# Linear attention and a gated block: the value projection per token becomes a product of moments, and biases become rows of weights

## The chip, the core and the metric

One NeuronCore of a Trainium2 runs the whole kernel. The metric is the device time of one execution in microseconds. TensorE is called PE in the profile, VectorE DVE, ScalarE ACT, GpSimd POOL, and SyncE (which issues the transfers here) SP. The engines run their own instruction streams in order and wait for each other on semaphores.

## What is computed

```python
xn = layernorm(x)                                   # x: 8 batches x 512 tokens x 128
q, k, v = split(xn @ Wqkv + bqkv, 3)
qp, kp = elu(q) + 1, elu(k) + 1
kv = einsum('bsd,bse->bde', kp, v)                  # one 128x128 matrix a batch
attn = (qp @ kv) / (qp . sum_s kp + 1e-6)
x1 = layer_norm(xn + attn, g1, b1)
s = layer_norm(x1 + (silu(x1 @ Wg + bg) * (x1 @ Wu + bu)) @ Wd + bd, g2, b2)

gf = global_net(mean_s xn)                          # three small layers on the mean over tokens
out = xn
for _ in range(3):                                  # coupling cycles
    tf = coupling_net(out)                          # 128 -> 128 -> 64 -> 32 -> 1, gelu
    c = 0.1 + adaptive_range * (0.7 * gf + 0.3 * tf - 0.5) * 2
    out = out + c * twist(out)                      # twist: quarters of the features swapped, some negated
result = x + s * silu(out)
```

## The kernel before

Everything stays on chip between the first load and the last store. A batch is four tiles of 128 tokens, so there are 32 tiles. Each engine has one hand-written order of work, and counters (semaphores, one for each product) tie them together. There are three stages.

**Token stage (to about 67 us).** For batch b, TensorE projects q for the whole batch (`project_q`, L890 to L894) and then, tile by tile (`project_tokens`, L903 to L906), k, v and two products with the first coupling weight, 512 columns in all. Float32 operands are split into a high and a low part, so each product is three matmuls, and the biases of k and v are one more matmul against a matrix of ones (L905). ScalarE reads each tile's bank in `token_tile`: exp for k (L373), the copy of v (L376), the copy of the other two quarters (L377). VectorE makes the k feature (`feature_k`, L578). TensorE then adds k feature times (v, 1) into one bank (`sum_kv`, L915), two tiles behind the projection. VectorE copies the sum (`copy_kv`, L585), TensorE multiplies the q features with it (`numerator`, L924), VectorE divides and adds xn (`attend`, L601), then takes the statistics of the sum (L527, L533) and negates the mean (`negate_mean`, L539). GpSimd adds epsilon (L228), takes the power -0.5 (L229) and forms minus mean times rstd (L240). ScalarE normalises (`norm_1`, L385) for batches 0 to 4, GpSimd (`norm_x1`, L257) for batches 5 to 7, and GpSimd multiplies with g1 into x1g (`scale_x1`, L265). For batches 6 and 7 that multiplication stands in GpSimd's order behind `s_pair` (L280, L281), four pairs of long products that belong to the coupling stage. TensorE transposes x1n (`transpose_x1`, L870 in the profile, as all transposes). Three banks serve the tiles in turn, so the projection of tile n waits for the k feature of tile n-3.

ScalarE's order within batch b is: exp of q; for each tile its `token_tile`; `norm_1` of two tiles of batch b-3 behind tiles 0 and 2; the high part of the next batch's transposed xn (`hi_x`, L360) behind tile 1; `hi_x1` at the end. The high and low parts of the transposed xn also accumulate its sum over tokens, from which the mean for the global net comes (L777).

**Coupling stage (to about 128 us).** Twelve slots, a slot being two batches in one of the three cycles: layers 1 to 4 on TensorE with gelu on ScalarE, then the coefficient (`coupling`, L625) and the next layer's input (`next_r`, L637, eight VectorE instructions) on VectorE. The second cycle of a slot reads what `s_pair` wrote.

**Second block (to the end).** For each batch, gate and up products (L1014 to L1016), silu on ScalarE (L446), their product on VectorE (L663), the down product (`down`, L1026) with a bias matmul in front of each tile (L1024, L1039), the residual with x1g and its statistics (L672, L527 to L539), the norm's scalars on GpSimd (L228 to L240), the norm on ScalarE (L454), three products of `gate_rows` on GpSimd (L313 to L317), `o3` on VectorE (L650), and `finish` (L698, L699) one or more batches behind. g1 is multiplied into the gate and up weights (L804), b1 and bd are in the bias matmul.

SP issues all loads in one order at the start: x of batch 0, the columns, the small weights, the first weights, x of batches 1 and 2, the rows, the gate and up weights, the down weights, x of batches 3 to 7. Each is spread over 128 partitions.

## Time and profile before

| | us |
|---|---|
| median of 3 runs | 209.87 |
| lowest and highest | 209.31, 210.67 |
| span of the profiled execution, first to last instruction | 208.3 |

| engine | busy us | share | instructions |
|---|---|---|---|
| TensorE matmul | 171.9 | 83% | 982 |
| VectorE | 168.9 | 81% | 535 |
| ScalarE | 116.5 | 56% | 288 |
| GpSimd | 135.7 | 65% | 220 |

The span lies 1.6 us under the median; what is around it (launch and end) is in the run's time and not in the span. In the timeline a row gives the start of an instruction and how long it was in its engine. Instructions of one engine overlap by their latency, so the price of one more in a full queue is the distance from its start to the next start, not its duration. A bracket at the end gives the idle time before the row and what ended it. PEclk is the TensorE clock granted, 1.00 being 2.4 GHz and 0.50 being 1.2 GHz.

### The profile page before, as it was taken

Reading aid. Unit: us, or ns where it says so; the run is one execution under the profiler, and the core shown is the slowest. Engines: PE = TensorE matmul, PEld = TensorE weight load, DVE = VectorE, ACT = ScalarE, POOL = GpSimd, SP = SyncE. Lnnn points to the kernel's source line nnn. Section 1 sums busy time; section 2 is a strip of 40 time slices with the busy share of each in tenths; the row PEclk is TensorE's granted clock in tenths of the full one; section 3 lists DMA queues with packets and bytes.
Section 4 is the critical chain, followed back from the end, with each engine's and each line's share of the span. In section 5 each row is a group of like instructions: output and inputs, shape, how many; then the busy total and the mean of one; then the engine's idle time right before and its main releaser. Section 6 shows DMA issues by size and latency. Waiting matters only on the chain.

```text
span 208.3 us, 3423 instructions
## 1 busy us (share of the span) xinstructions
PE 171.9 (83%) x982; PEld 119.9 (58%) x982; DVE 168.9 (81%) x535; ACT 116.5 (56%) x288; POOL 135.7 (65%) x220
## 2 busy tenths in 40 slices
PE   0399999999999899685959998669999979797900
PEld 0266776878677745342334545448788758585900
DVE  4865699999899945999995705984999999999864
ACT  2337687899888569545326886232374545343420
POOL 0284788799945994578671279981568466483981
PEclk9999999999999889979557999957999999999975
DMA  6950000000000000000000000000001011010112
GB/s 133 312 215 0 0 5 0 2 5 0 0 0 5 2 0 3 0 0 0 0 0 0 3 0 2 3 0 3 0 0 50 3 50 50 0 52 3 50 50 101
DMA packets 3330, 5.74 MB, mean 28 GB/s; under 512 B 496, under 2 KB 1136, under 8 KB 3312
## 3 DMA queue, kind: packets, MB, share of 16 engines
q1 hardware_dynamic: 3312, 5.52, 8.1%
q8 instruction: 8, 0.13, 0.3%
q14 instruction: 10, 0.08, 0.1%
HBM read 3.43 MB, written 2.10 MB: 27 GB/s over the span
## 4 chain that ended last, share of the span: by engine, by line
PE 51%; DVE 23%; ACT 8%; POOL 8%; issue 4%; DMA 2%; SPq 1%; DVEq 0%; ACTq 0%; POOLq 0%
DVE r_tok L637 9%; PE bank L1026 8%; DVE xn_tok L650 8%; PE bank L870 6%; PE bank L954 5%; PE bank L1014 4%; PE bank L1015 3%; PE bank L1016 3%; POOL rstd L229 3%; PE bank L966 2%; DMA r_tok<-in_w_first 2%; PE bank L903 2%; PE bank L906 2%; PE bank L904 2%; PE bank L915 2%
## 5 line engine op out<-in xcount | busy, mean ns | idle before, releaser
L228 POOL TENSOR_SCALAR ve<-mv 128x4 f32<-128x4 f32 (+1 forms) x25 | 5.1, 206 | 41.6 <-DVE nm L539 40.7
L1014 PE MATMUL bank<-x_hi,ffn_hi 128*128 128x512 f32 (+1 forms) x48 | 21.5, 448 | 9.2 <-DVE pq L663 8.2
L446 ACT ACTIVATE pq<-bank,bffn 128x512 f32<-128x512 f32 (+1 forms) x24 | 15.8, 680 | 21.4 <-PE bank L1016 21.4
L650 DVE SCALAR_TENSOR_TENSOR xn_tok<-tx_tok,ab,xn_tok 128x128 f32<-128x128 f32 x32 | 26.6, 888 | 0.0
L229 POOL TENSOR_TENSOR rstd<-ve,minus_half 128x4 f32<-128x4 f32 (+1 forms) x25 | 24.9, 998 | 2.1
L1026 PE MATMUL bank<-wd,pq 128*128 128x128 f32 x168 | 24.8, 295 | 0.0
L409 ACT ACTIVATE q_stage<-bank,col 128x512 f32<-128x512 f32 x24 | 16.4, 687 | 14.0 <-PE bank L870 13.4
L1026 PEld LDWEIGHTS bank<-wd,pq 128*128 128x128 f32 x168 | 22.5, 203 | 0.2
L663 DVE SCALAR_TENSOR_TENSOR pq<-bank,bffn,pq 128x512 f32<-128x512 f32 (+1 forms) x24 | 17.8, 745 | 4.5 <-ACT pq L446 4.2
L1015 PE MATMUL bank<-x_lo,ffn_hi 128*128 128x512 f32 (+1 forms) x48 | 19.4, 405 | 0.0
L1016 PE MATMUL bank<-x_hi,ffn_lo 128*128 128x512 f32 (+1 forms) x48 | 19.2, 401 | 0.0
L870 PE MATMUL bank<-small,r_tok 128*128 128x128 f32 x64 | 12.6, 330 | 7.7 <-DVE r_tok L637 7.7
L625 DVE SCALAR_TENSOR_TENSOR cpl<-tt,gain,base 128x8 f32<-128x8 f32 x12 | 6.7, 562 | 13.0 <-ACT tt L430 13.0
L637 DVE SCALAR_TENSOR_TENSOR r_tok<-pq,cpl 128x128 f32<-128x128 f32 x32 | 16.8, 594 | 0.1
L1014 PEld LDWEIGHTS bank<-x_hi,ffn_hi 128*128 128x128 f32 (+1 forms) x48 | 8.7, 182 | 14.3 <-DVE pq L663 10.6
L954 PE MATMUL bank<-q_stage,small 128*64 128x512 f32 x48 | 16.1, 755 | 0.0
L906 PE MATMUL bank<-first_hi,xT_lo 128*128 128x512 f32 x32 | 15.9, 497 | 0.0
L454 ACT ACTIVATE pq<-pq,nmr,rstd 128x128 f32<-128x128 f32 x28 | 11.5, 483 | 7.4 <-POOL nmr L240 7.4
L903 PE MATMUL bank<-first_hi,xT_hi 128*128 128x512 f32 x32 | 15.3, 479 | 0.0
L870 PEld LDWEIGHTS bank<-small,r_tok 128*128 128x128 f32 x64 | 8.5, 168 | 11.9 <-DVE r_tok L637 8.9
L373 ACT ACTIVATE ek<-bank,minus_one 128x128 f32<-128x128 f32 x32 | 12.1, 378 | 4.3 <-PE bank L906 3.1
L418 ACT ACTIVATE h<-bank,col 128x256 f32<-128x256 f32 x24 | 10.1, 470 | 7.7 <-PE bank L954 7.7
(134 smaller groups left out, 492.7 us busy)
## 6 DMA issues: line engine op xcount, KB each, us to landing
x_tok<-in_x SPq DMA_DIRECT2D x8, 256.0 KB, 6.4
out<-pq SPq DMA_DIRECT2D x7, 256.0 KB, 2.0
r_tok<-in_w_ffn SPq DMA_DIRECT2D x1, 341.0 KB, 6.3
r_tok<-in_w_first SPq DMA_DIRECT2D x1, 320.0 KB, 4.9
out<-pq SPq DMA_DIRECT2D x2, 128.0 KB, 1.8
small<-in_w_small SPq DMA_DIRECT2D x1, 242.0 KB, 4.1
row<-in_rows SPq DMA_DIRECT2D x1, 192.0 KB, 5.8
wd<-in_w_down SPq DMA_DIRECT2D x1, 192.0 KB, 6.3
```

The lines of the kernel that those rows point to most:

```text
L229: return pool.tensor_tensor(rstd[i][:, b, ts], ve[i][:, b, ts], minus_half[:, ts], ALU.pow)
L637: ins = dve.scalar_tensor_tensor(out=r_tok[:, n], in0=pq[:, n, 1], scalar=cpl[:, s, i // TILES, i % TILES:i % TILES + 1], in1=pq[:, n, 0] ...
L650: last = dve.scalar_tensor_tensor(out=xn_tok[:, b, t], in0=tx_tok[:, b, t], scalar=ab[:, j, 3, i:i + 1], in1=xn_tok[:, b, t], op0=ALU.mult ...
L663: dve.scalar_tensor_tensor(out=hid[b % 2][0:m, c], in0=ps_up[n % 2][0:m], scalar=bffn[0:m, CHUNKS + c:CHUNKS + c + 1], in1=sg[n % 2][0:m], ...
L870: last = pe.transpose(dst[:, t * P:(t + 1) * P], src[:, t], eye)
L903: pe.matmul(dst[:], hi, first_hi[:, 0:4 * D], start=True, stop=False)
L906: pe.matmul(dst[:], lo, first_hi[:, 0:4 * D], start=False, stop=True).then_inc(k_ps, 1)
L954: last = pe.matmul(ps_h2[s % 2][64 * par:64 * par + 64, :], sm("cn_w2"), h1[:, s % 2, par], start=True, stop=True)
L1014: pe.matmul(dst[n % 2][0:m], ffn_hi[:, w], x1_hi[:, b], start=True, stop=False)
L1015: pe.matmul(dst[n % 2][0:m], ffn_hi[:, w], x1_lo[:, b], start=False, stop=False)
L1016: pe.matmul(dst[n % 2][0:m], ffn_lo[:, w], x1_hi[:, b], start=False, stop=True).then_inc(done, 1)
L1026: last = pe.matmul(dst[:, t * P:(t + 1) * P], hid[b % 2][0:m, c, t * P:(t + 1) * P], wd[0:m, c], start=False, stop=(c == CHUNKS - 1))
```

## The change

- Value projection: v is no longer projected for each token. `project_tokens` has 384 columns (k and two coupling products) and the bias matmul 128. `sum_m` accumulates, for each batch, the product of xn (features 1 to 127 and a column of ones) with the k features (and a column of ones), one matmul a tile as before. Then VectorE copies this moment (`copy_m`), TensorE multiplies it with the prepared value weights (`project_kv`, one matmul a batch) and ScalarE copies the result (`copy_kv`), which stands in ScalarE's order behind tile 2 and its `norm_1`.
- The value weights are prepared once on VectorE (`value_weights`, at the end of batch 0): first row subtracted (xn sums to zero over its features), mean over outputs subtracted, so that the first norm's input has mean zero. The same for the first weights of the global net, which read the sum over tokens from the moment.
- The first norm is then a scale only. ScalarE scales for batches 0 to 4; VectorE makes x1g in one pass for batches 5 to 7 (`norm_x1`), and the x1n and x1g work of those batches leaves GpSimd. x1g is what is transposed, so the gate and up weights need no scaling. GpSimd loses the epsilon (all norms) and the product of mean and rstd (first norm); VectorE adds epsilon, which replaces the negated mean in norms 0 and 1 and is one more instruction in norm 2.
- bd and b1 become two rows of the down weights' last chunk (87 rows for 85), against ones that GpSimd writes into the hidden tiles; the bias matmuls of `down` go.
- Loads: the first weights in two transfers; five transfers for the value and global weights, four of them over 127 partitions and one a row of 128 single elements, placed ahead of the rows; the down weights in four, one over 85 partitions and two of them such rows.
- k features have four buffers for three; the accumulation of sums in `hi_x` and `lo_x` goes.

```diff
-                act.activation(xT_hi[:, b % 2], ps_xT[:], ACT.Identity,
-                               accum_out=sum_hi[:, b:b + 1]).then_inc(xT_hi_ready, 1)
+                act.copy(xT_hi[:, b % 2], ps_xT[:]).then_inc(xT_hi_ready, 1)
...
-                act.copy(v1[:, n % 3, 0:D], ps_k[n % 3][:, D:2 * D]).then_inc(v_ready, 1)
-                act.copy(pq[:, n].rearrange("p a d -> p (a d)"), ps_k[n % 3][:, 2 * D:4 * D]).then_inc(pq_ready, 1)
+                act.copy(pq[:, n].rearrange("p a d -> p (a d)"), ps_k[n % 3][:, D:3 * D]).then_inc(pq_ready, 1)
+
+            def copy_kv(b):
+                act.wait_ge(kv_ps, b + 1)
+                if b >= 2:
+                    act.wait_ge(num_ps, b - 1)
+                act.copy(kv_sb[:, b % 2], ps_kv).then_inc(kv_ready, 1)
...
                         norm_1(b - 3, (t, t + 1))
                     if t == 1 and b + 1 < BATCHES:
                         hi_x(b + 1)
+                    if t == 2 and b >= 1:
+                        copy_kv(b - 1)
...
-            def sum_kv(n):
+            def sum_m(n):
...
-                pe.matmul(ps_kv[:, 0:D + 1], kf[:, n % 3], v1[:, n % 3], start=(t == 0),
-                          stop=(t == TILES - 1)).then_inc(kv_ps, 1)
+                pe.matmul(ps_m, xn_ext[:, b, t, 1:D + 1], kf[:, n % KF], start=(t == 0),
+                          stop=(t == TILES - 1)).then_inc(m_ps, 1)
+
+            def project_kv(b):
+
+                pe.wait_ge(m_ready, b + 1)
...
+                pe.matmul(ps_kv, m_sb[:, b, 0:D], wv[:], start=True, stop=True).then_inc(kv_ps, 1)
...
-                    if n >= 2:
-                        sum_kv(n - 2)
+                    if t <= 1 and b >= 1:
+                        sum_m(n - 2)
                     if t == 1 and b + 1 < BATCHES:
                         transpose_x(b + 1)
-                    if t == 3 and b >= 1:
-                        numerator(b - 1)
...
+                    if t == 2 and b >= 1:
+                        project_kv(b - 1)
+                    if t == 3:
+                        sum_m(n - 3)
+                        sum_m(n - 2)
+                        if b >= 1:
+                            numerator(b - 1)
...
+            def value_weights():
+
+                dve.wait_ge(rest_cleared, 1)
+                dve.wait_ge(rest_loaded, 80)
+                link(dve.tensor_tensor(rest_raw, rest_raw, rest_base, ALU.subtract))
+                dve.tensor_copy(gw1[:], rest_raw[:, D:])
+                link(dve.bn_stats(st_v[:], rest_raw[:, 0:D]))
+                link(dve.bn_aggr(mv_v[:], st_v[:]))
+                dve.wait_ge(small_loaded, 16)
+                dve.tensor_copy(wv[:, D:D + 1], eye[:, P - 1:P])
+                dve.tensor_scalar(wv[:, 0:D], rest_raw[:, 0:D], mv_v[:, 0:1], None, ALU.subtract).then_inc(wv_ready, 1)
...
+            def norm_x1(b):
...
+                    last = dve.scalar_tensor_tensor(out=x1g[:, b, t], in0=u1[:, b % 2, t],
+                                                    scalar=rstd[1][:, b, t:t + 1], in1=row_g1,
+                                                    op0=ALU.mult, op1=ALU.mult)
...
-            for b in (BATCHES - 2, BATCHES - 1):
-                scale_x1(b)
...
-                link(pool.tensor_scalar(ve[i][:, b, ts], mv[i][:, b, ts, 1], 1.0, LN_EPS, ALU.mult, ALU.add))
...
+            sp.wait_ge(rest_cleared, 1)
+            gc = slice(SMALL_AT["gc_w1"], SMALL_AT["gc_w1"] + SMALL["gc_w1"])
+            sp.dma_start(rest_raw[0:P - 1, 0:D], w_first[1:P, D:2 * D]).then_inc(rest_loaded, 16)
+            sp.dma_start(rest_raw[P - 1:P, 0:D], as_row("bv"), allow_slow_non_contiguous=True).then_inc(rest_loaded, 16)
+            sp.dma_start(rest_raw[0:P - 1, D:], w_small[1:P, gc]).then_inc(rest_loaded, 16)
+            sp.dma_start(rest_base[0:P - 1, 0:D], w_first[0:1, D:2 * D].to_broadcast([P - 1, D])).then_inc(rest_loaded, 16)
+            sp.dma_start(rest_base[0:P - 1, D:], w_small[0:1, gc].to_broadcast([P - 1, NREST - D])).then_inc(rest_loaded, 16)
...
-                    pe.matmul(dst[:, t * P:(t + 1) * P], ones_bf[:, 0:P], bias3[:, 3 * D:4 * D], start=True, stop=False)
```

## Rows read from the trace of the kernel before

**Rows 1.** Busy time by window: busy us (instructions) of each engine, PEclk, DMA share, GB/s

```profile
40.00:50.00 10.00, 10.00 (x65) 7.49 (x63) 9.52 (x49) 9.27 (x31) 9.05 (x18) 1.00 0.01 3
```

**Rows 2.** Timeline, TensorE, batch 4 of the token stage: start us, us, instruction

```profile
39.09 0.40 PE L903 MATMUL bank<-first_hi,xT_hi 128*128 128x512 f32 x1
...
39.91 0.39 PE L915 MATMUL bank<-v,kf 128*128 128x129 f32 x2
...
43.71 1.06 PE L924 MATMUL bank<-kv_sb,q_stage 128*128 128x129 f32 x8
44.60 0.60 PE L870 MATMUL bank<-small,x1n 128*128 128x128 f32 x4
...
45.97 0.40 PE L903 MATMUL bank<-first_hi,xT_hi 128*128 128x512 f32 x1
```

**Rows 3.** Timeline, ScalarE, the same batch

```profile
40.11 0.37 ACT L373 ACTIVATE ek<-bank,minus_one 128x128 f32<-128x128 f32 x1
40.37 0.26 ACT L376 COPY v<-bank 128x128 f32<-128x128 f32 x1
40.52 0.39 ACT L377 COPY pq<-bank 128x256 f32<-128x256 f32 x1
40.78 0.89 ACT L385 ACTIVATE x1n<-u,nmr,rstd 128x128 f32<-128x128 f32 x2
41.57 0.37 ACT L373 ACTIVATE ek<-bank,minus_one 128x128 f32<-128x128 f32 x1
...
42.22 0.64 ACT L360 ACTIVATE xT_hi<-bank 128x512 fp32r<-128x512 f32 x1
...
42.80 0.41 ACT L373 ACTIVATE ek<-bank,minus_one 128x128 f32<-128x128 f32 x1
```

**Rows 4.** Timeline: TensorE at the start of batches 1 and 3

```profile
19.29 0.40 PE L903 MATMUL bank<-first_hi,xT_hi 128*128 128x512 f32 x1
...
32.20 0.39 PE L903 MATMUL bank<-first_hi,xT_hi 128*128 128x512 f32 x1
```

**Rows 5.** Timeline, VectorE: statistics of batch 3, last copy_kv, two gaps behind the stage

```profile
19.38 0.86 DVE L527 BATCH_NORM_STATS2 st<-x_tok 128x6 f32<-128x128 f32 x4
...
66.62 0.29 DVE L585 COPY kv_sb<-bank 128x129 f32<-128x129 f32 x1 [0.37 <-PE bank L915]
...
76.18 0.69 DVE L617 TENSOR_TENSOR x_lo<-bank,x_hi 128x512 fp32r<-128x512 f32 x1 [1.90 <-ACT x_hi L392]
...
79.06 0.23 DVE L625 SCALAR_TENSOR_TENSOR cpl<-tt,gain,base 128x8 f32<-128x8 f32 x1 [2.06 <-ACT tt L430]
```

**Rows 6.** Timeline, coupling slots 4 and 5: VectorE, then GpSimd, then TensorE

```profile
102.44 6.40 DVE L637 SCALAR_TENSOR_TENSOR r_tok<-pq,cpl,r_tok 128x128 f32<-128x128 f32 x8
...
109.02 2.19 DVE L637 SCALAR_TENSOR_TENSOR r_tok<-pq,cpl,r_tok 128x128 f32<-128x128 f32 x8
...
104.77 2.62 POOL L265 TENSOR_TENSOR x1g<-x1n,row 128x512 f32<-128x512 f32 x2
...
107.85 1.11 PE L870 MATMUL bank<-small,r_tok 128*128 128x128 f32 x4 [2.37 <-DVE r_tok L637]
...
113.00 0.64 PE L870 MATMUL bank<-small,r_tok 128*128 128x128 f32 x4
```

**Rows 7.** Timeline, second block: GpSimd's norm scalars and VectorE's finish

```profile
164.33 0.19 POOL L228 TENSOR_SCALAR ve<-mv 128x4 f32<-128x4 f32 x1 [3.28 <-DVE nm L539]
164.60 1.02 POOL L229 TENSOR_TENSOR rstd<-ve,minus_half 128x4 f32<-128x4 f32 x1
...
165.56 0.69 DVE L699 TENSOR_TENSOR pq<-pq,x_tok 128x512 f32<-128x512 f32 x1
...
165.70 0.62 POOL L240 TENSOR_TENSOR nmr<-nm,rstd 128x4 f32<-128x4 f32 x1
```

**Rows 8.** The page's transfer queue (packets, MB, share of 16 engines), and a window

```profile
q1 hardware_dynamic: 3312, 5.52, 8.1%
...
13.00:14.00 1.00, 1.00 (x4) 0.89 (x4) 0.69 (x1) 0.17 (x2) 0.93 (x3) 1.00 0.27 98
```

More of the change, by code:

```diff
@@ L248, in finish @@
                 pool.tensor_tensor(yb[b % 2], yb[b % 2], x_tok[:, b], ALU.add).then_inc(y_ready, 1)
-            def norm_x1(b):
-                pool.wait_ge(rstd_ready[1], b + 1)
-                pool.wait_ge(x1n_ready, b)
-                pool.wait_ge(x1T_ps, b - 1)
-                pool.wait_ge(x1g_ready, b - 1)
-                for t in range(TILES):
-                    last = pool.tensor_scalar(x1n[:, b % 2, t], u1[:, b % 2, t], nm[1][:, b, t:t + 1],
-                                              rstd[1][:, b, t:t + 1], ALU.add, ALU.mult)
-                last.then_inc(x1n_ready, 1)
             def scale_x1(b):
@@ L543, in stats @@
                 moments(i, b)
[L544 removed]
+                prepare_rstd(i, b)
             def stats_x(b):
@@ L774, in _ @@
                 feature_k(TILES * b)
-                if b == BATCHES - 1:
-                    dve.wait_ge(xT_lo_ready, BATCHES)
-                    dve.tensor_tensor(ctx_sum[:], sum_hi[:], sum_lo[:], ALU.add).then_inc(ctx_ready, 1)
                 if b >= 1:
-                    copy_kv(b - 1)
+                    copy_m(b - 1)
                 if b >= 2:
@@ L814, in _ @@
             invert_den(BATCHES - 2)
-            copy_kv(BATCHES - 1)
+            copy_m(BATCHES - 1)
             attend(BATCHES - 2)
+            norm_x1(ACT_NORMS)
             lo_x1(BATCHES - 4)
@@ L827, in _ @@
             stats_u1(BATCHES - 1)
+            norm_x1(BATCHES - 2)
             lo_x1(BATCHES - 3)
@@ L1056, in _ @@
             pe.wait_ge(split_ready, 1)
-            for i in range(4):
+            for i in range(2):
                 last = pe.transpose(ps_bias[0:3, i * D:(i + 1) * D], bias_split[:, i, 0:3], eye_bf[:])
```

235 lines of the change are left out of this document (133 added, 102 removed).

## The prediction, made before the changed kernel was run

> **What bounds the kernel now.** I read the page first: matmul and VectorE are each busy for over 80% of the span, which is an average over three stages with different limits. So I went by windows. In the middle of the token stage all four engines are full: matmul 10.00 of 10 us, VectorE 9.52, ScalarE 9.27, GpSimd 9.05, at the full clock [rows 1]. There, relief for one engine is worth only what the next one allows. Then I read the timelines of one batch. TensorE takes 6.88 us a batch, from 39.09 to 45.97, without a gap [rows 2]; ScalarE goes through its tiles in order [rows 3]. The chain of work that ended last and the waits led to the two other stages. In the coupling stage VectorE's `next_r` is on the chain, and it is slow exactly where GpSimd runs long products [rows 6]. In the second block VectorE and GpSimd hand work to each other [rows 7].
>
> All terms are made against the profiled span, 208.3 us; the median is 1.6 us above it, and I add the same change to the median.
>
> **TensorE in the token stage.** A tile is 3 x 512 + 256 = 1792 columns and takes 0.82 us, 39.09 to 39.91 [rows 2], so 0.46 ns a column. It loses 512 columns: 0.23 us a tile, 0.92 a batch. `project_kv` adds one matmul of the numerator's shape, a quarter of 0.89 (43.71 to 44.60 [rows 2]): 0.22. TensorE alone would need 6.88 - 0.92 + 0.22 = 6.18 us a batch.
>
> **Batches 0 to 2.** There ScalarE has no `norm_1`, so TensorE's own saving can show. Batch 0 gains 0.9 and no `project_kv`; batches 1 and 2, 12.91 us together now (19.29 to 32.20 [rows 4]), gain 0.7 each. Against it stands `value_weights` at the end of batch 0, six short instructions in VectorE's full order, in front of the statistics of batch 3 and the q feature of batch 1. The trace has none of them; the nearest row is the copy of 129 columns at 0.29 us [rows 5], which gives up to 1.7; below, 0, if VectorE's waits in batch 1 absorb them. I take 0.9, the middle. Batches 0 to 2: -0.9 - 1.4 + 0.9 = -1.4, between -2.3 and -0.6.
>
> **Batches 3 to 7: the wait that takes the place of the matmuls.** `numerator` waits for `copy_kv`, which moves from VectorE to ScalarE, behind the exp and copies of tiles 0 to 2, two pairs of `norm_1` and `hi_x`. Prices by start to start [rows 3]: exp 0.26, v 0.15, pq 0.26, two norms 0.79, `hi_x` 0.58 with its accumulator; I take 0.49 without. From the start of exp 0 the copy now ends after 0.51 + 0.79 + 0.50 + 0.49 + 0.50 + 0.79 + 0.29 (the copy, at VectorE's price [rows 5]) = 3.87 us. Exp 0 starts 0.20 behind its tile (39.91 to 40.11 [rows 2, 3]), the tile is 0.59, so the copy ends at 4.66 from the batch's start, 4.71 with a semaphore. TensorE would reach `numerator` at 4.62 - 0.92 + 0.22 = 3.92 (now 39.09 to 43.71 [rows 2]). It waits 0.79, and the batch is 6.18 + 0.79 = 6.97: not shorter than now. The wait holds up the transposes of x1 and the next q projection behind it. Batches 3 to 6 each lose 0.1. Batch 7 has no `hi_x` and gains 0.4. At the end `copy_m`, `project_kv` and `copy_kv` stand between the last sum and the global net, where before only `copy_kv` ran beside: 0.29 + 0.22 and two semaphores, +0.6. Together +0.6. If the copy came early enough the same batches would give 5 x 0.7 less the 0.6, -2.9; VectorE, 9.52 of 10 us busy [rows 1], would then hold back about half of it. Token stage: -1.4 + 0.6 = -0.8, between -4 and +0.7.
>
> **Norms moved to VectorE.** Three `norm_x1` of four two-input instructions, 0.27 each by the undisturbed `next_r` (2.19 / 8 [rows 6]), are 3.3 us. They stand between the statistics of batches 6 and 7 and the first coefficient, where VectorE now waits 1.90 and 2.06 us [rows 5]. I price them at nothing because of these 3.96 us; without that cover they would cost up to 3.3 on the way to the first `next_r`.
>
> **x1g leaves GpSimd's order in the coupling stage.** `next_r` of slot 4 took 6.40 us for eight instructions and of slot 5 2.19 [rows 6]. The second and third of slot 4 each wait for one of the two x1g products of 1.31 us, from 104.77 to 107.39 [rows 6], and the transposes wait for the fourth. Without the products the second to fourth run from 104.8 at 0.27 each, with some 0.1 of GpSimd's short ones between, and end at 105.7 instead of 107.8: -2.1, between -1.0 and -2.4. This is the largest single term. **Clock:** behind this gap of 2.37 us TensorE works at 1.2 GHz: four transposes 1.11 us at 107.85 against 0.64 at 113.00 [rows 6]. At that ratio the 5.2 us between these two rows would be 3.0 at the full level. The gap nearly closes, so the clock should come back sooner; between 0 and -2.2, I take -0.7.
>
> **Second block.** The bias matmuls of 128 columns are 0.06 us each by the price a column. Six lie before VectorE becomes the limit, some at 1.2 GHz, and four in `down_last`: -0.5. Each norm loses GpSimd's epsilon, 0.27 (164.33 to 164.60 [rows 7]), for a VectorE instruction of about 0.07: -0.2 where GpSimd is next. But now the product of mean and rstd arrives at 165.70, while `finish` holds VectorE and GpSimd apart from 165.56, and takes 0.62 [rows 7]. Coming 0.2 earlier it can slip in between the two `finish` products and push the second, and with it `gate_rows`, back by 0.2. Two batches without `finish` gain 0.2, four lose 0.2: +0.4, between -1.2 and +2.5. The end of the kernel gains 0.3 from the epsilon of the last two norms. Second block: -0.5 + 0.4 - 0.3 = -0.4.
>
> **Start.** The first weights are 256 KB instead of 320, in two transfers; one more issue against fewer bytes, 0 within 0.4. The columns of ones, the shorter splits and the memsets lie beside the loads.
>
> **Sum.** -0.8 - 2.1 - 0.7 - 0.4 = -4.0: span 204.3, median 205.9 us.
>
> **Rivals.** *A. The narrow loads come late (slower).* Four of the five new loads go over 127 partitions and all stand ahead of x of batches 3 to 7. If such a load is not spread but goes through one of the 16 transfer engines, that engine has 4 x 127 = 508 rows of 384 B on average, 195 KB. The trace has only loads over 128 partitions: 3312 packets took 8.1% of 16 x 208.3 us, 270 us, so 81.5 ns and 1.67 KB a packet [rows 8]. By bytes that makes 9.6 us, by packets 41. The rows are small; I take 13. The engine begins them at about 7 us, when the x of batches 0 to 2 is in (in the kernel before everything is in by 14 [rows 8]); with 1 us of landing and 4 of the other loads, x of batch 3 would land at 25 where its statistics are wanted at about 18.4 (19.38 now [rows 5] less the gain). Less 1 us of slack in batch 1 that is +5 to +6, so about 211; by the two ends, +2 to +33. It makes the kernel slower by 1% from +6.1 on, when the 508 rows take over some 14 us. For it: the new shapes. Against: nothing of the kind is in the trace. The Trainium skill, in DMA: Bandwidth & Descriptors, section "Why a DMA increments its semaphore by 16 and not by 1", says that a transfer uses the largest number of engines up to 16 that divides its partitions, and one for 127; no run here shows it yet. By that rule this rival's condition holds, and only the price of a small row is open. Chance 0.32.
> *B. ScalarE's order does not hold `numerator` back* (its single-input scaling is cheaper, or VectorE's lag hides the copy): the stage gives -3 and not -0.8, 203.7 us. For it, v's copy leaves ScalarE; against, the sum above. Chance 0.12.
> *C. The gain is eaten* by `value_weights`, the uncovered norms or the collisions of GpSimd and VectorE in the second block at their upper ends: +0.8, +1 and +1.5 on the forecast, about 209. Chance 0.13.
> The forecast case has 0.43.
>
> **How the numbers follow.** The forecast case runs from 203 to 208, B down to 202, C up to 210.5, A mostly from 207 to 214. The range 202 to 212.5 leaves out about 0.05 below and 0.12 above. Within 1% is what a measurement of this kernel can hardly tell from no change; 1% is 2.1 us, so faster means under 207.8 and slower over 212.0. Faster: 0.38 of the forecast case, 0.12 of B, 0.02 of C, 0.05 of A: 0.57. Same: 0.05 + 0.10 + 0.12 = 0.27. Slower: 0.01 of C, 0.15 of A: 0.16.
>
> **What the new profile would show.** TensorE starts batch 3 near 30.8 and its batches then keep about 7 us, with a gap in front of `numerator` released by ScalarE's copy; without that gap B is right. VectorE has no wait on a transfer in batch 0; one of several us there means A. The `next_r` of slot 4 takes about 4.4 us and the transposes follow it at full clock soon after. In the second block the distance between two negated means stays near 9.2 us. The prediction falls if a load or the moved norms stand on the chain, or if batches 3 to 6 are under 6.5 us.

## The result, and the profile after

The changed kernel takes 226.72 us (median of 4 runs, 225.22 to 228.12), the kernel before on the same chip 209.59 (208.81 to 210.67). The ratio is 1.089, with a 95% interval of 1.075 to 1.103. The forecast was 205.9 us with a range up to 212.5: wrong in sign and in size. The profiled execution has a span of 226.2 us against 208.3, 17.9 more. The times below are medians of all runs of a kernel; these spread by up to 3.6%, the slower ones mostly at a lower granted clock, and the profiled executions of e1_wide, e2_x1n and b1_x1g are slower ones.

Where the 17.9 us are is read from a few marks that both timelines have:

| stretch | before | after | difference |
|---|---|---|---|
| start to the q projection of batch 0 | 10.26 | 9.31 | -0.95 |
| to that of batch 7 | 48.87 | 66.03 | +17.16 |
| to ScalarE's table load behind the token stage | 7.75 | 11.32 | +3.57 |
| to the first `next_r` | 12.4 | 14.1 | +1.7 |
| to `next_r` of slot 4 | 23.1 | 23.1 | 0.0 |
| to the last `next_r` | 14.7 | 13.2 | -1.5 |
| to the end | 91.1 | 89.1 | -2.0 |

So the token stage and what follows at once lost 21.5 us, and the two later stages won 3.5. (The table compares one execution with one.) The middle of the token stage, by windows, after (busy us and instructions of PE, PEld, DVE, ACT, POOL; granted clock; share and GB/s of the transfers), where [rows 1] had 10.00, 7.49, 9.52, 9.27 and 9.05:

```profile
50.00:60.00 10.00, 6.72 (x47) 5.43 (x46) 6.37 (x33) 5.18 (x17) 7.26 (x12) 1.00 0.01 2
```

No engine is full any more. They wait for each other. The first q matmul of each batch on TensorE (timeline, after: start us, us, instruction), to be read beside the 6.88 us of a batch in [rows 2]:

```profile
9.31 0.79 PE L939 MATMUL bank<-xT_hi,first_hi 128*128 128x512 f32 x1 [0.67 <-ACT xT_hi L384]
16.14 0.48 PE L939 MATMUL bank<-xT_hi,first_hi 128*128 128x512 f32 x1
28.98 0.78 PE L939 MATMUL bank<-xT_hi,first_hi 128*128 128x512 f32 x1
35.91 0.48 PE L939 MATMUL bank<-xT_hi,first_hi 128*128 128x512 f32 x1
45.65 0.47 PE L939 MATMUL bank<-xT_hi,first_hi 128*128 128x512 f32 x1
...
75.34 0.47 PE L939 MATMUL bank<-xT_hi,first_hi 128*128 128x512 f32 x1
```

Two things are to be seen. Batch 1 takes 12.84 us, once, and is followed by a matmul at 0.78 instead of 0.48 us: the granted clock was 0.50 from 28.98 to 30.00. And from batch 3 on the distance is 9.74, 10.15, 10.16 and 9.38.

**Batch 1: the loads.** The issues on SP's queue (timeline, after; the second number is how long the issue held the queue), and then VectorE and TensorE in batch 1:

```profile
3.53 0.43 SPq L218 DMA_DIRECT2D x_tok<-in_x  x1
4.00 0.33 SPq L221 DMA_DIRECT2D r_tok<-in_w_first  x1
4.38 3.70 SPq L222 DMA_DIRECT2D r_tok<-in_cols  x1
8.13 0.44 SPq L223 DMA_DIRECT2D r_tok<-in_w_small  x1
8.61 2.48 SPq L224 DMA_DIRECT2D r_tok<-in_w_first  x1
11.13 1.76 SPq L225 DMA_DIRECT2D r_tok<-in_w_small  x1
12.93 2.92 SPq L226 DMA_DIRECT2D row<-in_rows  x1
...
18.41 2.49 SPq L234 DMA_DIRECT2D x_tok<-in_x  x5
...
22.21 0.87 DVE L554 BATCH_NORM_STATS2 st<-x_tok 128x6 f32<-128x128 f32 x4 [2.88 <-DMA x_tok<-in_x]
...
24.75 0.80 PE L974 MATMUL bank<-wv,m_sb 128*128 128x129 f32 x2 [4.59 <-DVE m_sb L611]
```

Ordinary issues take 0.43 us. Of the five behind the first narrow load, four take 3.70, 2.48, 1.76 and 2.92, and x of batch 3 is issued at 18.4. VectorE waits 2.88 us for it during TensorE's batch 1, `copy_m` stands behind that wait in its order, and TensorE waits 4.59 us for `m_sb`.

**Batches 3 to 7: a ring.** One round, from batch 4 to 5, after, on the four engines (timeline), and the waits of the whole execution (engine, tile and line waited for: us in total, times, longest):

```profile
47.15 0.37 DVE L560 BATCH_NORM_AGGREGATE mv<-st 128x2 f32<-128x6 f32 x4
47.56 0.17 DVE L568 TENSOR_SCALAR ve<-mv 128x4 f32<-128x4 f32 x1
...
47.81 1.01 POOL L260 TENSOR_TENSOR rstd<-ve,minus_half 128x4 f32<-128x4 f32 x1 [2.63 <-DVE ve L568]
48.92 3.13 POOL L265 TENSOR_SCALAR xn_ext<-x_tok,mv,rstd 128x128 f32<-128x128 f32 x4
52.02 1.09 POOL L294 TENSOR_SCALAR tx_tok<-xn_ext 128x128 f32<-128x128 f32 x4
53.08 1.03 POOL L260 TENSOR_TENSOR rstd<-ve,minus_half 128x4 f32<-128x4 f32 x1
54.08 1.26 POOL L288 TENSOR_TENSOR x1g<-x1n,row 128x512 f32<-128x512 f32 x1
...
55.39 0.66 PE L919 MATMUL bank<-small,x1g 128*128 128x128 f32 x4 [2.60 <-POOL x1g L288]
...
56.09 0.59 ACT L416 CAST x_hi<-bank 128x512 fp32r<-128x512 f32 x1 [4.48 <-PE bank L919]
...
56.70 0.69 DVE L656 TENSOR_TENSOR x_lo<-bank,x_hi 128x512 fp32r<-128x512 f32 x1 [3.59 <-ACT x_hi L416]
57.31 0.37 DVE L560 BATCH_NORM_AGGREGATE mv<-st 128x2 f32<-128x6 f32 x4
```

```profile
ACT x_hi L416 <- PE bank L919: 20.5, 5, 4.5
...
DVE x_lo L656 <- ACT x_hi L416: 15.3, 5, 4.4
...
PE bank L919 <- POOL x1g L288: 11.1, 5, 2.6
```

From one `mv` to the next, 47.15 to 57.31, each row starts about when the one above it ends. GpSimd makes x1g last in its round; TensorE transposes x1g now, where it transposed x1n [rows 2]; ScalarE and VectorE wait for the transposes; and VectorE makes the moments of x for GpSimd's next round behind `lo_x1`. The ring closes in 10.16 us.

### The profile page after: what moved, and what is told of

It reads as the page before. It is cut to its first block, busy times and chain, and to the rows that moved or that the text cites. A ratio compares the mean times of both kernels' runs of the same rounds, so it can differ in the third digit from the quotient of the medians.

```text
span 226.2 us, 3307 instructions
## 1 busy us (share of the span) xinstructions
PE 171.3 (76%) x961; PEld 124.5 (55%) x964; DVE 167.2 (74%) x551; ACT 109.6 (48%) x256; POOL 128.6 (57%) x175
## 4 chain that ended last, share of the span: by engine, by line
PE 36%; DVE 27%; POOL 17%; SPq 7%; issue 4%; ACT 4%; DMA 2%; DVEq 0%; ACTq 0%; POOLq 0%
DVE xn_ext L689 8%; DVE r_tok L676 7%; PE bank L919 7%; PE bank L1083 5%; POOL rstd L260 4%; POOL xn_ext L265 4%; PE bank L1012 4%; PE bank L1072 3%; POOL x1g L288 3%; DVE pq L704 3%; PE bank L1073 2%; PE bank L1074 2%; PE bank L1024 2%; DVE cpl L664 2%; DVE st L554 2%
## 5 line engine op out<-in xcount | busy, mean ns | idle before, releaser
L689 DVE SCALAR_TENSOR_TENSOR xn_ext<-tx_tok,ab,xn_ext 128x128 f32<-128x128 f32 x32 | 25.3, 850 | 0.0
L265 POOL TENSOR_SCALAR xn_ext<-x_tok,mv,rstd 128x128 f32<-128x128 f32 x28 | 21.9, 795 | 0.8
L1083 PE MATMUL bank<-wd,pq 128*128 128x128 f32 x168 | 22.3, 285 | 0.0
L919 PE MATMUL bank<-small,r_tok 128*128 128x128 f32 x64 | 12.0, 316 | 7.0 <-DVE r_tok L676 7.0
L656 DVE TENSOR_TENSOR x_lo<-bank,x_hi 128x512 fp32r<-128x512 f32 x8 | 5.5, 687 | 15.3 <-ACT x_hi L416 15.3
L664 DVE SCALAR_TENSOR_TENSOR cpl<-tt,gain,base 128x8 f32<-128x8 f32 x12 | 6.8, 563 | 12.5 <-ACT tt L454 12.5
L1012 PE MATMUL bank<-q_stage,small 128*64 128x512 f32 x48 | 15.3, 720 | 0.0
L416 ACT CAST x_hi<-bank 128x512 fp32r<-128x512 f32 x8 | 4.7, 585 | 20.5 <-PE bank L919 20.5
L478 ACT ACTIVATE pq<-pq,nmr,rstd 128x128 f32<-128x128 f32 x28 | 11.5, 482 | 6.2 <-POOL nmr L274 6.2
L966 PE MATMUL bank<-kf,xn_ext 128*128 128x129 f32 x64 | 11.8, 290 | 3.3 <-ACT kv_sb L403 3.2
L303 POOL TENSOR_TENSOR pq<-pq,cpl 128x1024 f32<-128x1024 f32 x4 | 7.6, 1896 | 11.7 <-DVE r_tok L676 11.7
L919 PEld LDWEIGHTS bank<-small,r_tok 128*128 128x128 f32 x64 | 7.9, 160 | 11.2 <-DVE r_tok L676 8.9
```

What stands on the lines that cost most here:

```text
L265: last = pool.tensor_scalar(xn_tok[:, b, t], x_tok[:, b, t], mv[0][:, b, t, 0:1], rstd[0][:, b, t:t + 1], ALU.subtract, ALU.mult)
L689: last = dve.scalar_tensor_tensor(out=xn_tok[:, b, t], in0=tx_tok[:, b, t], scalar=ab[:, j, 3, i:i + 1], in1=xn_tok[:, b, t], op0=ALU.mult ...
L919: last = pe.transpose(dst[:, t * P:(t + 1) * P], src[:, t], eye)
L1012: last = pe.matmul(ps_h2[s % 2][64 * par:64 * par + 64, :], sm("cn_w2"), h1[:, s % 2, par], start=True, stop=True)
L1083: last = pe.matmul(dst[:, t * P:(t + 1) * P], hid[b % 2][0:m, c, t * P:(t + 1) * P], wd[0:m, c], start=(c == 0), stop=(c == CHUNKS - 1))
```

## The experiments

The distances between the first q matmuls of batches 1 to 7, read from each profiled execution, carry most of the argument. The last two columns are the median of the runs and that of the kernel before on the same chip.

| kernel | 1-2 | 2-3 | 3-4 | 4-5 | 5-6 | 6-7 | first `next_r` | median | before |
|---|---|---|---|---|---|---|---|---|---|
| before | 6.45 | 6.47 | 6.88 | 6.88 | 6.89 | 7.28 | 79.3 | 209.9 | |
| after | 12.84 | 6.93 | 9.74 | 10.15 | 10.16 | 9.38 | 100.8 | 226.7 | 209.6 |
| e1_wide | 6.84 | 6.34 | 10.03 | 10.97 | 10.16 | 10.96 | 97.2 | 220.6 | 208.8 |
| e1b_rows | 11.09 | 6.61 | 9.74 | 10.16 | 10.17 | 9.37 | 98.7 | 225.3 | 208.8 |
| e1c_split | 7.01 | 6.32 | 10.05 | 10.15 | 10.17 | 9.38 | 95.0 | 220.8 | 208.7 |
| e2_x1n | 13.04 | 6.77 | 7.34 | 7.35 | 7.36 | 8.23 | 90.3 | 212.9 | 208.8 |
| e3a_nm_add | 13.44 | 6.99 | 9.38 | 9.62 | 9.39 | 9.38 | 97.4 | 223.6 | 208.8 |
| e3b_mean_sub | 10.47 | 6.33 | 9.81 | 11.58 | 10.61 | 9.38 | 101.7 | 227.7 | 209.7 |
| e6_reorder | 12.16 | 7.13 | 9.74 | 9.40 | 9.39 | 9.36 | 96.6 | 225.9 | 208.7 |
| e7b_pool_order | 11.31 | 6.46 | 8.74 | 9.18 | 9.17 | 7.34 | 88.5 | 216.8 | 209.7 |
| e7_both_orders | 11.10 | 6.81 | 8.73 | 7.51 | 8.03 | 7.34 | 85.9 | 213.4 | 209.7 |
| b1_x1g | 6.43 | 6.47 | 11.01 | 12.48 | 11.75 | 12.50 | 108.4 | 236.9 | 208.7 |
| e5n_no_ckv | 6.88 | 6.33 | 7.34 | 7.35 | 7.36 | 7.35 | 79.0 | 206.0 | 209.7 |
| e5_all | 6.88 | 6.33 | 6.77 | 6.77 | 6.77 | 6.89 | 78.2 | 204.4 | 208.7 |
| e9_orders_all | 7.01 | 6.33 | 7.41 | 7.26 | 7.24 | 7.25 | 78.8 | 205.9 | 207.9 |
| e10_ffn_early | 6.87 | 6.32 | 6.77 | 6.76 | 6.76 | 6.77 | 75.7 | 203.7 | 207.9 |

Theory X says that the ring through x1g is the main loss, theory L that the late loads are (rival A of the prediction).

### The loads: e1_wide, e1b_rows, e1c_split

e1_wide packs the narrow pieces into tensors of 128 rows:

```diff
-            sp.dma_start(rest_raw[0:P - 1, 0:D], w_first[1:P, D:2 * D]).then_inc(rest_loaded, 16)
-            sp.dma_start(rest_raw[P - 1:P, 0:D], as_row("bv"), allow_slow_non_contiguous=True).then_inc(rest_loaded, 16)
...
+            sp.dma_start(r_flat[:, 4 * D:4 * D + 2 * NREST], w_rest).then_inc(rest_loaded, 16)
...
+            sp.dma_start(wd[:], w_down).then_inc(down_loaded, 16)
```

> The changed kernel with its narrow loads undone: the value and global weights (shifted rows, bias row, base row) and the down weights with bias rows bd and b1 come in two transfers over all 128 partitions, at the same places in the order of issues. Theory L (the loads late are the main loss): the matmuls start batch 1 about 4.6 us earlier, nothing else is slow, so 226.7 falls to about 207. Theory X (a loop over the engines through x1g is the main loss, 17 us behind it): VectorE's wait of 2.88 us for x[3] and TensorE's of 4.59 us for m_sb go, batch 3 starts near 32.5 instead of 36.9, but batches 4 to 7 stay 10 us apart: about 222 (221 to 223).

220.64 us, 1.056 of before (1.049 to 1.063): 6.1 us less than the changed kernel. The wait for x of batch 3 and the 4.59 us are gone, batch 1 takes 6.84, and batches 3 to 6 stay at 10 to 11. Theory X holds, with 1.4 us more for the loads than it said. (Two of its distances, 10.97 and 10.96, are longer than in e1c_split below, 10.15 and 9.38; nothing here rests on them.)

e1b_rows reads the three bias rows from one piece of 512 bytes each instead of 128 single elements:

```diff
-            return cols[:, COL[name]:COL[name] + 1].rearrange("p a -> a p")
+            return bias_rows[i:i + 1]
```

> The changed kernel with one thing else: the three bias rows (bv, bd, b1) are read from a tensor in which each is 512 bytes in one piece, instead of 128 single elements 92 bytes or so apart; the transfers of 127 partitions stay. If the single elements hold the queue: the issue of 3.70 us falls to about 0.1, the four issues behind it lose most of their 7.6 us, x[3] comes 8 us earlier, and the time falls by 3 to 5 us (about 222.5). If the 127 partitions are what is slow: the issues behind stay near 2 us each, the data for value_weights come as late as before, 226.

225.33 us (two runs, 223.75 and 226.92), which can't be told from 226.72. The single elements are not it; the issues stay long (timeline, e1b_rows):

```profile
4.38 3.14 SPq L223 DMA_DIRECT2D r_tok<-in_bias_rows  x1
...
7.86 2.73 SPq L225 DMA_DIRECT2D r_tok<-in_w_first  x1
```

e1c_split cuts each transfer of 127 partitions in one of 112 and one of 15 and leaves the single elements:

```diff
-            sp.dma_start(rest_raw[0:P - 1, 0:D], w_first[1:P, D:2 * D]).then_inc(rest_loaded, 16)
+            for lo, hi in ((0, 112), (112, P - 1)):
+                sp.dma_start(rest_raw[lo:hi, 0:D], w_first[lo + 1:hi + 1, D:2 * D]).then_inc(rest_loaded, 16)
```

> The changed kernel with each transfer of 127 partitions (two of weights, two of the base row) cut in two, of 112 and of 15 partitions; the single-element rows stay as they are. If a transfer of 127 partitions is what fills a queue (all its rows on one of the 16 engines): the issues of 3.70, 2.48, 1.76 and 2.92 us fall below 0.6 each, x[3] is issued near 11 instead of 18.4, VectorE's wait of 2.88 for x[3] goes. If the number of transfers or of small rows is what fills it, the issues stay as long or grow, and x[3] is issued at 18 or later.

Four more transfers, and all issues are short (timeline, e1c_split):

```profile
4.00 0.95 SPq L222 DMA_DIRECT2D r_tok<-in_w_first  x2
5.00 0.57 SPq L223 DMA_DIRECT2D r_tok<-in_cols  x1
...
11.48 2.49 SPq L237 DMA_DIRECT2D x_tok<-in_x  x5
```

(`x2` and `x5` stand for two and five issues in one row.) The same single-element row now takes 0.57 us to issue, x of batch 3 is issued at 11.5 instead of 18.4, and the one run took 220.81 us, as e1_wide. So it was the number 127. It would be explained if all 127 rows go through one transfer engine, whose queue is then full and holds SP. The issues that take long are those behind the narrow ones, the full-width `row` at 12.93 too. The Trainium skill, in DMA: Bandwidth & Descriptors, section "Why a DMA increments its semaphore by 16 and not by 1", gives one engine for 127 partitions and 16 for 128; these three runs agree with it. That one engine did the work is argued from it; no view here shows the engines apart.

### The ring: e2_x1n, e3a, e6, e7b, e7 and b1

e2_x1n transposes x1n again for batches 0 to 4 and applies g1 where the transposed tile is read:

```diff
-                transposes(ps_x1T, x1g[:, b]).then_inc(x1T_ps, 1)
+                transposes(ps_x1T, x1n[:, b % 2] if b < ACT_NORMS else x1g[:, b]).then_inc(x1T_ps, 1)
...
+                    ins = act.activation(x1_hi[:, b], ps_x1T[:], ACT.Identity, scale=col[:, COL["g1"]:COL["g1"] + 1])
...
+                    ins = dve.scalar_tensor_tensor(out=x1_lo[:, b], in0=ps_x1T[:], scalar=col[:, COL["g1"]:COL["g1"] + 1],
+                                                   in1=x1_hi[:, b].bitcast(F32), op0=ALU.mult, op1=ALU.subtract)
```

> The changed kernel, but for batches 0 to 4 TensorE transposes x1n, as the kernel before did, and g1 is applied per partition by the two readers of the transposed tile (ScalarE's high part with g1 as scale, VectorE's low part as multiply and subtract); GpSimd's x1g is then off the path. Theory X: the waits of 1.8 to 2.6 us before the transposes go, and 4.1 to 4.5 of ScalarE and 3.3 to 4.4 of VectorE behind them; the distance of the batches falls from 10.1 to 7.3 to 7.8, five times 2.5: about 214 (212 to 217). Theory L: nothing of it is on the path, 226. If another loop holds the batches, GpSimd's own work (7.3 us busy in 10), the distance stays over 8.5: 219.

212.91 us, but the four runs spread from 207.6 to 215.0, so 12 to 19 us less than the changed kernel. The distances are 7.35, and by the first `next_r` 10.5 us are won (90.3 against 100.8). Theory L falls: the ring's share is won while batch 1 still takes 13.04.

e3a_nm_add gives GpSimd its old norm back; e3b_mean_sub keeps the subtraction but takes the mean from consecutive columns:

```diff
-                    last = pool.tensor_scalar(xn_tok[:, b, t], x_tok[:, b, t], mv[0][:, b, t, 0:1],
-                                              rstd[0][:, b, t:t + 1], ALU.subtract, ALU.mult)
+                    last = pool.tensor_scalar(xn_tok[:, b, t], x_tok[:, b, t], nm[0][:, b, t:t + 1],
+                                              rstd[0][:, b, t:t + 1], ALU.add, ALU.mult)
```

> The changed kernel with GpSimd's norm of x in its old form: x plus a negated mean from its own tile (a copy of 4 columns on VectorE for it), in place of x minus the mean read from every second column of mv. If the operand or the operation makes the 794 ns: the mean of one falls to about 450, GpSimd's round by 1.4 us, and as its round is part of the loop the time falls by 5 to 7 us: about 220.5. If the rows of 129 elements make it, it stays at 794 and the time at 226 to 227.

> The changed kernel with GpSimd's norm of x still a subtraction, but of a mean copied into its own tile of consecutive columns. Settles what made 795 ns of 448: if it is the mean read from every second column of mv, the mean of one falls to about 448; if it is subtract in place of add, it stays at 795.

223.62 us (two runs) and 227.65 (one run). The groups of instructions by line (busy us, mean ns of one) of the changed kernel, then of e3a_nm_add, then of e3b_mean_sub:

```profile
L265 POOL TENSOR_SCALAR xn_ext<-x_tok,mv,rstd 128x128 f32<-128x128 f32 x28 | 21.9, 795 | 0.8
```

```profile
L265 POOL TENSOR_SCALAR xn_ext<-x_tok,nm,rstd 128x128 f32<-128x128 f32 x28 | 12.2, 448 | 0.8
```

```profile
L265 POOL TENSOR_SCALAR xn_ext<-x_tok,nm,rstd 128x128 f32<-128x128 f32 x28 | 21.9, 795 | 0.8
```

The rows of 129 elements and the strided mean cost nothing; subtract in place of add does, 347 ns an instruction. But the distances fell only to 9.4, where the ring less 1.4 us would be 8.7, and the time by 3.1 where 5 to 7 were expected (the intervals of the two ratios, 1.061 to 1.083 and 1.075 to 1.103, overlap). Something else holds at 9.4.

e6_reorder cuts the ring on VectorE (in batches 3 and 4, where both pieces stand):

```diff
+                if b + 3 < BATCHES:
+                    moments(0, b + 3)
+                    prepare_rstd(0, b + 3)
                 if 3 <= b < BATCHES - 1:
                     lo_x1(b - 3)
-                if b + 3 < BATCHES:
-                    moments(0, b + 3)
-                    prepare_rstd(0, b + 3)
```

> The changed kernel with one order on VectorE altered: in batches 3 and 4, where both stand, the moments and the variance of x[b+3] are made before lo_x1(b-3), not behind it. The loop theory: x1g, transposes, x_hi, x_lo, moments, ve, power, norm, twist, power, x1g form a closed chain through four engines, whose rows sum to 1.26 + 0.60 + 0.69 + 0.69 + 0.37 + 0.17 + 1.03 + 3.13 + 1.09 + 1.03 = 10.1 us, the distance of the batches. Cut between x_lo and the moments, GpSimd starts its norm some 3 us earlier in batches 3 and 4: their distances fall to about 7.5 to 8, later ones stay (no norm is left in them): 4 to 6 us less, about 221. The plain theory (GpSimd is simply late, whatever comes before it): no change, 226.

225.87 us, and again 9.4. The miss is the useful one. Its timeline of batch 4 (e6_reorder):

```profile
51.50 0.17 DVE L568 TENSOR_SCALAR ve<-mv 128x4 f32<-128x4 f32 x1
...
51.76 1.03 POOL L260 TENSOR_TENSOR rstd<-ve,minus_half 128x4 f32<-128x4 f32 x1 [1.88 <-DVE ve L568]
52.76 1.26 POOL L288 TENSOR_TENSOR x1g<-x1n,row 128x512 f32<-128x512 f32 x1
...
54.07 0.66 PE L919 MATMUL bank<-small,x1g 128*128 128x128 f32 x4 [1.84 <-POOL x1g L288]
```

The norm is over early, and GpSimd waits 1.88 us for another variance, that of u1 of two batches back (`rstd_1(b - 2)`), which VectorE makes only behind the k features of TensorE's present batch. `scale_x1` stands behind that power in GpSimd's order, the transposes behind `scale_x1`, the next batch's tiles behind the transposes. This second ring takes 6.4 us from the batch's first matmul to the variance (45.08 to 51.50), 1.3 for the power, 1.3 for x1g and 0.4 for the transposes, which is the 9.4. It had been hidden behind the first.

e7b_pool_order changes the order on GpSimd alone, e7_both_orders both:

```diff
-                if b >= 2:
-                    rstd_1(b - 2)
                 if 3 <= b < ACT_NORMS + 3:
                     scale_x1(b - 3)
+                if b >= 2:
+                    rstd_1(b - 2)
```

> The changed kernel with one order on GpSimd altered: scale_x1(b-3) stands ahead of rstd_1(b-2), not behind it. Theory of two chains: one through norm, twist, power and x1g (10.15 us, less the power of 1.03: 9.1 while norms are left, batches 3 to 5), one through the token tiles, the variance of u1(b-2), its power and x1g (9.4), which this edit cuts; from batch 6 on neither holds and the distance is 7.4. The distances of 9.74, 10.15, 10.16 and 9.38 become about 8.7, 9.1, 9.1 and 7.4: 5 to 6 us less, 221. If there is but the first chain: 1.0 less in each of three, 223.5.

> The changed kernel with both orders altered: VectorE's moments of x[b+3] ahead of lo_x1(b-3) (which alone left 225.9 and distances of 9.4), and GpSimd's scale_x1(b-3) ahead of rstd_1(b-2). TensorE still transposes x1g. Theory of two chains: each edit alone leaves the other chain, together none holds; GpSimd's own round (7.4) and TensorE's (6.7 and 0.7 for kv) then set the distance, 7.4 to 7.8: 10 us less in all, 216 (214 to 218). If the dependence on GpSimd as such is the price, whatever its order: 222 to 226.

e7b: 216.77 us (two runs), 10 us less by moving one call. Its distances of 8.74, 9.18, 9.17 and 7.34 are those foretold from the two rings; the total fell further than foretold (221): from the last q projection to the table load it takes 8.80 us for 11.32, and from there to the first `next_r` 10.87 for 14.11, where eight numerator matmuls take 1.14 us and not 2.07, at 2.4 GHz and not at 1.2. e7: 213.44 (two runs; 1.018, 1.014 to 1.022), below the 214 to 218 expected; distances 8.73, 7.51, 8.03, 7.34, where 7.4 to 7.8 were. In the 8.73 TensorE still waits 1.18 us for x1g (at 42.97). Otherwise GpSimd's own round, 1.0 + 3.1 + 1.1 + 1.3 + 1.0 = 7.5 us with the subtract in it, and the wait for kv (0.68) are left.

b1_x1g puts the one dependence into the kernel before: for batches 0 to 4 TensorE transposes x1g (g1 is then applied twice, so that factor of the output differs).

```diff
-                pe.wait_ge(x1n_ready, b + 1)
+                pe.wait_ge(*((x1g_ready, b + 1) if b < ACT_NORMS else (x1n_ready, b + 1)))
...
-                transposes(ps_x1T, x1n[:, b % 2]).then_inc(x1T_ps, 1)
+                transposes(ps_x1T, x1g[:, b] if b < ACT_NORMS else x1n[:, b % 2]).then_inc(x1T_ps, 1)
```

> The kernel before with one dependence of the change: for batches 0 to 4 TensorE transposes x1g, which GpSimd makes last, instead of x1n (g1 is then applied twice, so the output differs in that factor). If the closed chain is the cause it is so here too: 1.30 + 0.60 + 0.69 + 0.69 + 0.36 + 0.25 + 0.28 + 1.10 + 1.74 + 1.10 + 0.28 + 1.10 + 0.20 = 9.7 us against a distance of 6.88 now, in four or five batches: +11 to +14, about 221. If the chain only holds the changed kernel because its norm on GpSimd is slow: +0 to +3, 211.

236.85 us (two runs), 28 more, twice what was expected: distances of 11 to 12.5. The 9.7 was the first ring alone. Here the second is the longer one: from 40.84 to 53.32 it takes 8.6 us to the negated mean (49.48), 1.8 for GpSimd's scalars, 1.3 for x1g and 0.8 for the transposes. Part of it is the clock: four transposes take 1.11 us at 52.55, 0.66 at 40.43. The dependence by itself, in the orders of the kernel before, costs more than the whole change lost.

### All of it undone: e5_all, e5n_no_ckv, e9_orders_all, e10_ffn_early

e5_all is e1_wide with e2_x1n, e3a_nm_add, and `copy_kv` ahead of the second half of `norm_1`; e5n_no_ckv is the same without that last edit:

```diff
+                    if t == 2 and b >= 1:
+                        copy_kv(b - 1)
                     if t in (0, 2) and b >= 3:
                         norm_1(b - 3, (t, t + 1))
                     if t == 1 and b + 1 < BATCHES:
                         hi_x(b + 1)
-                    if t == 2 and b >= 1:
-                        copy_kv(b - 1)
```

> The changed kernel with four things undone together: wide transfers, x1n transposed with g1 in its two readers, GpSimd's norm with the negated mean from its own tile, and copy_kv on ScalarE ahead of the second half of norm_1. The sum of the forecast holds then, as nothing else was left out: distance of the batches 6.6 to 6.8 (7.35 in the run with x1n alone, less TensorE's 0.69 for kv), coupling stage begins near 78 to 79 (79.3 in the kernel before), coupling stage and second block keep what they won (1.6 and 2.0 us): 205 (203 to 207). If more is hidden in the token stage (queues behind sum_m on TensorE, an engine whose order is too tight), it begins at 82 or later: 209.

> The kernel of the run with all four undone, but with copy_kv back behind the second half of norm_1, as the change has it. If the wait of 0.68 before the first numerator matmul is a cost a batch: distances of 7.3 to 7.4 in place of 6.77, five times 0.6: 3 us more than 204.4, 207.4. If norm_1's second half then takes its place (x1n later, transposes wait): no difference, 204.4.

e5_all: 204.41 us, 0.982 of before (0.972 to 0.992); e5n: 205.97 (two runs; 0.982, 0.979 to 0.985). The distances are 6.77 against 7.35: the wait for kv costs 0.6 a batch, as expected. In the whole time 3 us were expected and 1.6 came, between two chips; by their ratios, both 0.982, the two kernels can't be told apart. Of the 2.4 us that e5_all was ahead at the table load (65.70 against 68.08), it gave 1.6 back before the first `next_r` (12.51 us against 10.87): eight numerator matmuls took 2.07 us there (68.88) and 1.14 in e5n (71.07), the clock at 1.2 GHz in the one and 2.4 in the other, behind a wait for `m_sb` in batch 7 of 1.16 us in e5_all and 0.23 in e5n. That the wait lowered the clock is argued, not shown.

That wait is what e10_ffn_early takes away: VectorE's FFN weights in batches 1 and 2 instead of 5 and 6, on top of e5_all. e9_orders_all asks the other open question: all mended, but x1g still transposed, with both orders of e7. The edit shown is that of e10.

```diff
-                if b == 5:
+                if b == 1:
                     dve.wait_ge(ffn_loaded, 16)
...
-                if b == 6:
+                if b == 2:
                     dve.wait_ge(ffn_step, 1)
```

> The changed kernel with wide transfers, GpSimd's norm in the add form, copy_kv ahead of the second half of norm_1 and both orders altered (VectorE's moments of x[b+3] ahead of lo_x1, GpSimd's scale_x1 ahead of rstd_1); TensorE still transposes x1g, as the change has it. If the orders alone made the dependence on x1g dear: GpSimd's round is 1.0 + 1.8 + 1.1 + 1.3 + 1.0 = 6.2 of 6.8 us, so the distances fall to 6.8 to 7.2, 205 to 206, within 1% of the 204.4 of the run that transposes x1n. If x1g cannot arrive in time even then (x1n is ready only after the second half of norm_1, x1g 1.3 us later, TensorE idle meanwhile): distances 7.5 to 8.0, 208 to 210.

> The kernel of the run with all four undone, and VectorE's copy and rest of the FFN weights made in batches 1 and 2 instead of 5 and 6, where the rest took 1.88 us and m_sb came late for it (TensorE waits 1.16 us for m_sb in batch 7). If that wait is a cost: the last batch shortens by about 1.2 and the time falls from 204.4 to about 203.2. If batches 1 and 2 have no room on VectorE (7.7 and 8.4 of 10 us busy), the same is lost there: 204.4.

e9: 205.94 us, 0.984 (0.977 to 0.992); its distances, 7.24 to 7.41, are a little over the 6.8 to 7.2 expected, its time is within the 205 to 206. TensorE's waits for x1g, five in e9, have shrunk from 11.1 us to 1.4 (waits, e9_orders_all):

```profile
PE bank L910 <- POOL x1g L279: 1.4, 5, 0.4
```

So most of the price was not in the dependence on x1g as such but in the places of two calls; what is left of it is some 0.5 us a batch (7.25 against the 6.77 of e5_all). e10: 203.67 us (6 runs), 0.978 (0.973 to 0.984), the fastest, about 23 us below the change as it stood. The stretch from the last q projection to the table load fell from 9.42 to 8.21, the expected 1.2, and the next one, to the first `next_r`, from 12.51 to 10.86, with the eight numerator matmuls again at 1.14 us. Of these 2.9 us 0.7 show between the two medians, taken on different chips, which is within their spread; in the profiled executions e10's second block is 1.3 us longer.

## Why the prediction was wrong, point by point

**The step that failed: the transposes.** The sum names the numerator's wait and says that it "holds up the transposes of x1", but nothing in it prices that the transposes now read x1g. Among the edits, x1g appears only as "x1g leaves GpSimd's order in the coupling stage", where it is a gain. In the token stage it is the reverse: the last product of GpSimd's round, off the path before, goes onto it. The rows were there: GpSimd was busy for 9.05 of 10 us [rows 1]. Batches 3 to 6 were forecast at 6.97 us and took up to 10.16. Undoing this alone gave back 12 to 19 us (e2_x1n), moving one call of GpSimd 10 (e7b). A transposed tile that GpSimd makes last should have been followed around all engines: the ring is 10.16 us long, where the sum had 6.97.

**Rival A came true beside it.** Its condition (127 partitions are not spread) fits what e1b_rows and e1c_split show, and its sign appeared: in VectorE's batch 0 the statistics wait 2.88 us for a transfer. It had x of batch 3 wanted at 18.4 and landed at 25, a loss of 5 to 6; the statistics ran at 22.21, and the loss was 6.1 (e1_wide). What it did not name is the way: the narrow loads hold SP's issue of everything behind them. It had a chance of 0.32 and a time of 211; e2_x1n, which keeps the late loads and lacks only the ring, took 212.9 in the median, 207.6 to 215.0. The two together gave what no case held.

**GpSimd's norm** was not priced: the change turned its add into a subtract, which took 795 ns instead of 448. Undone alone it gave 3.1 us, hardly clear of the spread and less than its 1.4 a batch, since the second ring then holds.

**The numerator's wait** was right in place and size: 0.79 forecast, 0.68 measured, released by ScalarE's copy. It falls on the `sum_m` just ahead of `numerator`. After (waits):

```profile
PE bank L966 <- ACT kv_sb L403: 3.2, 5, 0.7
```

What was mis-sized is TensorE's own batch: 6.18 forecast, 7.35 - 0.68 = 6.67 measured with the wait and 6.77 without it. A tile was to win 0.23 us, 512 columns at 0.46 ns. The second tile of a batch, before and in e5_all (timeline, TensorE):

```profile
40.05 0.48 PE L903 MATMUL bank<-first_hi,xT_hi 128*128 128x512 f32 x1
...
40.60 0.28 PE L905 MATMUL bank<-bias,ones_bf 128*128 128x256 bf16 x1
40.64 0.48 PE L906 MATMUL bank<-first_hi,xT_lo 128*128 128x512 f32 x1
40.96 0.38 PE L915 MATMUL bank<-v,kf 128*128 128x129 f32 x2
```

```profile
51.19 0.42 PE L955 MATMUL bank<-first_hi,xT_hi 128*128 128x384 f32 x1
...
51.63 0.23 PE L957 MATMUL bank<-bias,ones_bf 128*128 128x128 bf16 x1
51.67 0.42 PE L958 MATMUL bank<-first_hi,xT_lo 128*128 128x384 f32 x1
51.93 0.38 PE L968 MATMUL bank<-kf,xn_ext 128*128 128x129 f32 x2
```

It takes 0.91 us before and 0.74 in e5_all. The first tile takes 0.82 and 0.65 (50.40 to 51.05), so each wins 0.17: the three float32 products lose 128 columns each, at the 0.46 ns of the forecast. What it had wrong is the bias matmul, which takes 0.04 us from its start to the next with 256 columns and with 128, so its 128 columns gave nothing. That is 0.06 of 0.23 in each of four tiles, 0.2 a batch. A second part is the order: in e2_x1n the two sums that now stand together ahead of `numerator` take 0.52 us (49.39 to 49.91), where two single ones took 0.14 and 0.22.

**Start and batches 0 to 2.** Forecast 0 and -1.4. With the loads mended (e10) the q projection of batch 0 starts at 9.16, not 10.26, and that of batch 3 is 20.4 us later, not 20.9: -1.1 and -0.5. `value_weights` took 1.4 us in the changed kernel (17.94 to 19.34), in its bounds.

**x1g leaves the coupling stage.** Forecast -2.1; after (timeline, VectorE, then TensorE behind it), against the 6.40 of [rows 6]:

```profile
123.88 4.36 DVE L676 SCALAR_TENSOR_TENSOR r_tok<-pq,cpl,r_tok 128x128 f32<-128x128 f32 x8
...
127.24 1.12 PE L919 MATMUL bank<-small,r_tok 128*128 128x128 f32 x4 [1.62 <-DVE r_tok L676]
...
132.94 0.64 PE L919 MATMUL bank<-small,r_tok 128*128 128x128 f32 x4
```

-2.04: right, with the sign named beforehand (4.4). **The clock term behind it**: the gap did not nearly close but shrank from 2.37 to 1.62 us, the transposes still run at 1.2 GHz (1.12 us against 0.64), and the stretch to the first at 2.4 GHz is 5.70 us where it was 5.15. Forecast -0.7, measured +0.5 in this execution; so -1.5 in all. It isn't so in every one: in e2_x1n and e9_orders_all the granted clock is 1.00 at this place, and from `next_r` of slot 5 to that of slot 6 it is 3.0 us (117.92 to 120.93, 106.44 to 109.45) where it is 5.30 in the changed kernel and 4.93 before. From the first `next_r` to the last it takes 33.9 us there and up to 38.0 in e3a_nm_add and e6_reorder (before 37.8, after 36.3), with the same code in this stage. So the sign of the clock term stays open, and -1.5 is less than what the clock alone moves.

**The norms moved to VectorE** were priced at nothing. In e10, which has them, the stretch from the table load to the first `next_r` is 10.9 us against 12.4 before, so nothing is seen of them. The +1.7 in the changed kernel goes, in part at least, with the clock (0.50 granted there): eight transposes at 86.51 take 1.97 us, in e5_all at 65.52 1.09.

**Second block.** Forecast -0.4, measured -2.0 (the last `next_r` to the end). Bias matmuls, epsilon and end are right in sign; the term of the collision was mis-sized and has the wrong sign. After (timeline, GpSimd and VectorE), against [rows 7]:

```profile
176.67 0.20 POOL L274 TENSOR_TENSOR nmr<-nm,rstd 128x4 f32<-128x4 f32 x1
...
176.05 0.68 DVE L739 TENSOR_TENSOR pq<-pq,tx_tok 128x512 f32<-128x512 f32 x1
176.77 0.69 DVE L740 TENSOR_TENSOR pq<-pq,x_tok 128x512 f32<-128x512 f32 x1
```

The product does slip in between the two `finish` products, as the prediction feared. But there it takes 0.20 us instead of 0.62 and delays neither, and the distance of the negated means falls from 9.15 to 8.75, four times: -1.6 where +0.4 was said. The one distance before these four grew by 0.7 (7.37 to 8.09), and the end, behind the last of them, is 0.85 shorter where 0.3 was said.

**The sum.** With what it left out put right, the forecast's own terms give 205.9; e9 measured 205.94, e5n 205.97 (0.984 and 0.982 of before, forecast 0.981). That agreement is partly luck: the token stage won less per batch and more at the start, the second block more, and the clock's share differs from execution to execution.
